# Moving a feed-forward in front of a top-k selection, into the loop of the norm before it

## What is computed

```python
h = h + attention(layernorm(h))
n = layernorm(h)
weights = n @ wr + br                        # one number per token
idx = top_k(weights, S // 2)[:S // 2 - 1]    # per batch element
y = gelu(n[idx] @ w1 + b1) @ w2 + b2         # 64 -> 256 -> 64
processed = zeros_like(n).at[idx].set(y * weights[idx])
out = h + processed + n
```

## Time and profile before

| | us |
|---|---|
| median of 3 runs | 5121.56 |
| lowest and highest | 5119.72, 5126.37 |
| the profiled execution | 5121.87 |
| its span | 5120.3 |
| second norm, selection, feed-forward within it | 242.6, 68.2, 263.8 |

### The profile page before, as it was taken

The page is one execution under the profiler, slowest core; times in us unless marked ns, Lnnn a source line. Parts: engine busy times, 40 slices in busy tenths (PEclk is TensorE's granted clock), DMA queues, the critical chain, the costliest instruction groups (busy, mean ns, idle before and its releaser), DMA issues. The chain is left out here.

```text
span 5120.3 us, 108154 instructions
## 1 busy us (share of the span) xinstructions
PE 4427.8 (86%) x42924; PEld 1534.1 (30%) x42924; DVE 3914.3 (76%) x4567; ACT 3520.9 (69%) x7159; POOL 592.9 (12%) x1086
## 2 busy tenths in 40 slices
PE   8888874999999889999998999999899999956366
PEld 2333321333333323333332333333233333311122
DVE  3444446899899879989997998999799899954511
ACT  4444440888888778888887888888788788832133
POOL 1222220100110010010001101100100010012100
PEclk9999985999999999999998999999899999977688
DMA  4333322000100010010001001000100100024233
GB/s 126 97 101 92 97 78 71 20 8 6 38 10 6 8 38 8 6 36 10 8 6 38 10 6 35 10 8 6 38 8 8 33 13 7 7 84 143 64 101 104
DMA packets 178692, 203.94 MB, mean 40 GB/s; under 512 B 55372, under 2 KB 138620, under 8 KB 177916
## 3 DMA queue, kind: packets, MB, share of 16 engines
q1 hardware_dynamic: 175444, 192.19, 13.7%
q10 hardware_dynamic: 2736, 4.76, 0.3%
HBM read 116.96 MB, written 79.02 MB: 38 GB/s over the span
## 5 line engine op out<-in xcount | busy, mean ns | idle before, releaser
L883 DVE TENSOR_REDUCE part_max<-max_scores 128x2 f32<-128x1024 f32 (+3 forms) x3096 | 3228.2, 1101 | 372.6 <-PE max_scores L841 270.3
L1011 ACT ACTIVATE probs<-scores 128x512 f32<-128x512 f32 (+4 forms) x6272 | 2997.7, 538 | 548.3 <-PE scores L1041 439.6
L1065 PE MATMUL out_acc<-probs,v_keys 128*32 128x256 f32 (+2 forms) x23424 | 1790.5, 378 | 0.0
L841 PE MATMUL max_scores<-k_rows,q_rows 48*128 48x512 bf16 (+5 forms) x6416 | 1148.3, 370 | 186.0 <-DVE part_max L883 116.0
L1041 PE MATMUL scores<-q_rows,k_rows 50*128 50x512 bf16 (+4 forms) x6272 | 1216.1, 354 | 92.1 <-ACT probs L1011 44.1
L991 POOL TENSOR_SCALAR_AFFINE_SELECT probs<-probs 128x256 f32<-128x256 f32 (+1 forms) x832 | 334.5, 402 | 3422.5 <-ACT probs L1011 3420.6
L841 PEld LDWEIGHTS max_scores<-k_rows,q_rows 48*128 48x128 bf16 (+1 forms) x6416 | 303.1, 94 | 1298.9 <-DVE part_max L883 762.9
L1065 PEld LDWEIGHTS out_acc<-probs,v_keys 128*32 128x32 f32 x23424 | 463.2, 108 | 736.5 <-issue 622.9
L1041 PEld LDWEIGHTS scores<-q_rows,k_rows 50*128 50x128 bf16 x6272 | 469.8, 94 | 435.2 <-ACT probs L1011 226.2
L570 ACT ACTIVATE gate<-gate_ps,b_sb 128x448 f32<-128x448 f32 x252 | 148.1, 631 | 285.9 <-PE gate_ps L483 265.3
L848 PE MATMUL max_scores<-masks_sb 64*128 64x128 bf16 (+2 forms) x3424 | 220.1, 207 | 0.0
(11 more groups left out here) (122 smaller groups left out, 2239.4 us busy)
## 6 DMA issues: line engine op xcount, KB each, us to landing
q_terms_dram<-q_st SPq DMA_DIRECT2D x168, 112.0 KB
q_rows<-q_terms_dram SPq DMA_DIRECT2D x180, 96.0 KB, 2.2
v_keys<-v_blocks_dram SPq DMA_DIRECT2D x18, 832.0 KB, 9.5
v_blocks_dram<-v_st SPq DMA_DIRECT2D x24, 512.0 KB, 3.5
x_taps<-in_x SPq DMA_DIRECT2D x96, 116.0 KB, 2.9
k_rows<-k_terms_dram SPq DMA_DIRECT2D x36, 306.0 KB, 7.1
k_terms_dram<-k_st SPq DMA_DIRECT2D x168, 56.0 KB
h_dram<-h SPq DMA_DIRECT2D x28, 224.0 KB, 2.0
```

Source lines behind the costliest of these rows:

```text
L841: last = nc.tensor.matmul(max_scores[to:to + m, n % M_RING, v, 0:keys], q_rows[rows, g, p, q0:q0 + m], k_rows[rows, (u // BU) % STEP_B, g, ...
L883: nc.vector.tensor_reduce(part_max[0:m, u % 2, i, :, p, c], max_scores[0:m, n % M_RING, :, 0:keys], AX_X, ALU.max).then_inc(max_used, 1)
L1011: nc.scalar.activation(probs[0:keys, k % P_RING, s, o:width[t]], scores[0:keys, (GH * k + s) % S_RING, o:width[t]], ACT.Exp, scale=float(H ...
L1065: last = nc.tensor.matmul(out_acc[VW * s:VW * s + VW, lo:hi], v_keys[0:keys, u // BU, g, j, v * VW:(v + 1) * VW], probs[0:keys, k % P_RING ...
```

## The change

The two loops of two steps become one unrolled loop over all 28 tiles, and the feed-forward goes into it. `second_norm` becomes `second_half`: it no longer stores `normed` and `total`; `total` stays in SBUF for all tiles (`total_all`), and the Gelu and both products of the feed-forward are done while the tile is there. The first product now takes 64 rows of each half, without zeros. Its result with the bias stays in SBUF too (`y_all`). The router's bias moves from ACT to DVE, the weights are stored tile by tile, and the constants' loads come behind those of the first two tiles. `proj_ps`, `var_ps` and `router_ps` go from two buffers to one. `select` is the same. `apply_chosen` takes the place of `feed_forward`: `chosen` comes in eight large loads ahead of all stores, DVE multiplies and adds, PE turns, ACT copies, SP stores.

```diff
+        hidden = sbuf("hidden3", [P, 2, 2, 2, TILE])
+        proj_ps = psum("proj2_ps", [P, TILE])
         centred_ps = psum("centred2_ps", [P, 2, TILE])
+        var_ps = psum("var2_ps", [P, TILE])
+        router_ps = psum("router_ps", [2, TILE])
+        hidden_ps = psum("hidden3_ps", [P, 2, TILE])
+        y_ps = psum("y3_ps", [P, TILE])
...
+            def _(sp):
...
+                load(0)
+                load(1)
...
+                for dst, src in pieces:
+                    sp.dma_start(dst, src).then_inc(const_in, 16)
+                for m in range(2, RING):
+                    load(m)
+                for m, (q, t0, w) in enumerate(ALL_TILES):
+                    if m + RING < NT:
+                        load(m + RING)
+                    sp.wait_ge(router_set, m + 1)
+                    sp.dma_start(weights_out[2 * q:2 * q + 2, t0:t0 + w], router[:, m % RING, 0:w]).then_inc(router_out[m % RING], 16)
...
+                def first(m, half):
+
+                    w = ALL_TILES[m][2]
+                    pe.wait_ge(normed_ready, m + 1)
+                    for e in range(2):
+                        n = 4 * m + 2 * half + e
+                        if n >= 2:
+                            pe.wait_ge(gelu_ready, n - 1)
+                        nc.tensor.matmul(hidden_ps[:, e, 0:w], w1_sb[C * e:C * (e + 1), half],
+                                         normed[C * e:C * (e + 1), m % RING, 0:w],
+                                         start=True, stop=True).then_inc(hidden_ready, 1)
+
+                def second(m):
+                    w = ALL_TILES[m][2]
+                    if m >= 1:
+                        pe.wait_ge(y_set, m)
...
+                pe.wait_ge(const_in, 16 * CONSTS)
+                project(0)
+                centre_tile(0)
+                project(1)
+                for m in range(NT + 2):
+                    if m < NT:
+                        variance(m)
+                    if 1 <= m <= NT:
+                        first(m - 1, 0)
+                    if m + 1 < NT:
+                        centre_tile(m + 1)
+                    if m + 2 < NT:
+                        project(m + 2)
+                    if m >= 2:
+                        second(m - 2)
+                    if 1 <= m <= NT:
+                        first(m - 1, 1)
+                        route(m - 1)
...
+                squares(0)
+                for m in range(NT + 1):
+                    if m < NT:
+                        deviation(m)
+                    if m >= 1:
+                        gelu(m - 1, 0)
+                    if m + 1 < NT:
+                        squares(m + 1)
+                    if m >= 1:
+                        gelu(m - 1, 1)
...
+                def take_up(m):
+                    q, t0, w = ALL_TILES[m]
+                    dve.wait_ge(y_ready, m + 1)
+                    nc.vector.tensor_scalar(y_all[:, q, t0:t0 + w], y_ps[:, 0:w], b2_sb[:], None, ALU.add).then_inc(y_set, 1)
+
+                def weigh(m):
+                    w = ALL_TILES[m][2]
+                    dve.wait_ge(router_ready, m + 1)
+                    if m >= RING:
+                        dve.wait_ge(router_out[m % RING], 16 * (m // RING))
+                    nc.vector.tensor_scalar(router[:, m % RING, 0:w], router_ps[:, 0:w], br_sb[:], None, ALU.add).then_inc(router_set, 1)
...
+                    if m + 2 < NT:
+                        residual(m + 2)
+                    if m >= 2:
+                        take_up(m - 2)
+                    if 1 <= m <= NT:
+                        weigh(m - 1)
...
+def apply_chosen(nc, y_all, total_all, chosen_in, identity, out):
...
+        MIDDLE = 4 * TILE
...
+            def _(sp):
+                for q in range(PAIRS):
+                    for part, (a, b) in enumerate(((0, MIDDLE), (MIDDLE, S))):
+                        rows = chosen_in[2 * q:2 * q + 2][:, None, a:b]
+                        sp.dma_start(chosen[:, q, a:b], rows.to_broadcast([2, C, b - a])).then_inc(loaded[2 * q + part], 16)
...
+                for m, (q, t0, w) in enumerate(ALL_TILES):
+                    r = m % RING
+                    sp.wait_ge(turned_set, m + 1)
+                    k, rest = divmod(w, P)
+                    for e in range(2):
+                        rows = out[2 * q + e]
+                        sp.dma_start(rows[t0:t0 + k * P].rearrange("(k p) c -> p k c", p=P),
+                                     turned[:, r, 0:k, e * C:(e + 1) * C]).then_inc(stored[r], 16)
...
+                    dve.wait_ge(loaded[2 * q + (t0 >= MIDDLE)], 16)
+                    nc.vector.tensor_tensor(scaled[:, m % 2, 0:w], y_all[:, q, t0:t0 + w], chosen[:, q, t0:t0 + w],
+                                            ALU.mult).then_inc(scaled_ready, 1)
...
+                    act.wait_ge(turned_ready, m + 1)
+                    if m >= RING:
+                        act.wait_ge(stored[r], stored_by(m, r))
```

More of the change, by code:

```diff
@@ L1185, in second_norm @@
         router_set = sem("router_set")
[L1186 to L1237, removed]
-                        if m >= 2:
[L1239 to L1269, removed]
-                        nc.gpsimd.tensor_tensor(attn[:, m % 2, 0:w], heads[:, r, 0:w], inv[:, r, 0:w],
-                                                ALU.mult).then_inc(attn_ready, 1)
-                    def add(m):
-                        w = STEP_TILES[m][2]
-                        r, left, count = tile_out(m)
-                        pool.wait_ge(normed_ready, m + 1)
-                        if m >= RING:
-                            pool.wait_ge(left, count)
-                        nc.gpsimd.tensor_tensor(total[:, r, 0:w], normed[:, r, 0:w], h2[:, r, 0:w],
-                                                ALU.add).then_inc(total_ready, 1)
-                    multiply(0)
-                    multiply(1)
-                    for m in range(NT):
-                        if m + 2 < NT:
-                            multiply(m + 2)
-                        if m >= 1:
-                            add(m - 1)
-                    add(NT - 1)
-                @block.vector
-                def _(dve):
-                    def residual(m):
-                        w = STEP_TILES[m][2]
-                        dve.wait_ge(proj_ready, m + 1)
-                        r, landed, count = tile_in(m)
-                        dve.wait_ge(landed, count)
-                        if m >= RING:
-                            dve.wait_ge(total_ready, m - RING + 1)
-                            dve.wait_ge(centred, m - RING + 1)
-                        nc.vector.tensor_tensor(h2[:, r, 0:w], proj_ps[:, m % 2, 0:w], h0[:, r, 0:w],
-                                                ALU.add).then_inc(h2_ready, 1)
-                    residual(0)
-                    residual(1)
-                    for m in range(NT):
-                        w = STEP_TILES[m][2]
@@ L1522, in feed_forward @@
         turned_set = sem("turned3_set")
-        stored = [sem("out3_stored_even"), sem("out3_stored_odd")]
-        step_sems = [*loaded, hidden_ready, gelu_ready, y_ready, scaled_ready, final_ready, turned_ready,
-                     turned_set, *stored]
-        NT = len(STEP_TILES)
+        stored = [sem(f"out3_{r}_stored") for r in range(RING)]
+        NT = len(ALL_TILES)
         def stores(m):
-            w = STEP_TILES[m][2]
+            w = ALL_TILES[m][2]
             return 2 * ((w >= P) + (w % P > 0))
-        def stored_by(m, half):
-            return 16 * sum(stores(n) for n in range(m) if n % 2 == half)
@@ L1680, in program @@
     inverse_sums(nc, heads, inverse)
[L1681 to L1683 removed]
+    with nc.sbuf_tensor("y_all", [P, PAIRS, S], F32) as y_all, nc.sbuf_tensor("total_all", [P, PAIRS, S], F32) as total_all:
+        second_half(nc, heads, inverse, h0, a["wo"], a["wr"], a["br"], (a["centre"], a["mean"]),
+                    (a["ff_w1"], a["ff_w2"]), (a["ff_b1"], a["ff_b2"]), y_all, total_all, weights)
+        select(nc, weights, a["batch_sum"], a["batch_before"], chosen)
+        apply_chosen(nc, y_all, total_all, chosen, a["identity"], out)
 def arranged(i):
@@ L1735, in arranged @@
     same = at[:, None] // ROWS_PER_BATCH == at[None, :] // ROWS_PER_BATCH
-    ff_w1 = np.zeros((2, C, CHUNKS, P), np.float32)
-    for e in range(2):
-        for half in range(2):
-            ff_w1[e, :, 2 * e + half] = i["L0_ffn_w1"][:, half * P:(half + 1) * P]
     return {
```

402 lines of the change are left out of this document (185 added, 217 removed).

## The result

The changed kernel takes 5004.6 us, median of 4 runs (5003.3 to 5006.9), against 5120.9 us: a ratio of 0.977, 95% interval 0.976 to 0.979. The forecast was 5006 us. The profiled run took 5004.5 us, span 5002.4 us.

A forecast was written before the change was run, and what follows sets the result against it. A queue round of loads and stores bound the second norm, two DMA engines the feed-forward. Span 5120.3 - 20.6 (loop) - 94.8 (last stage) = 5004.9 us, with 1.57 us above span 5006 us; its own range 4973 to 5046.

The forecast's parts named there:

- Bound of the second norm: Second norm before the change: a queue round of POOL's add, SP's store, next load and POOL's multiply, 8.54 us per tile.
- bound of the feed-forward: Feed-forward before the change: loads of `chosen` run on two DMA engines, 8.1 us per full tile, 207 of 263.8 us.
- Last stage, 169 us: Stage after selection: loads 129 us plus stores 31.5 us on two engines, plus ends; 169 us against 263.8, gain 94.8.
- the line through two packet sizes: Last stage's loads: packet cost 9.8 ns + 0.0371 ns a byte, from 256 B and 2048 B packets; 129 us in all.
- 31.5 + 8: Last stage beyond its loads: stores 31.5 us, then 1 us to first byte, 3 us ring refill, 4 us last copy and store.
- The loop, 222 us: Merged loop: PE sets 7.2 us a full tile, 5.0 a short one, 193 us plus ends; 222 against 242.6, gain 20.6.
- Start and end: Loop outside its rounds: 18.8 us to the first variance, some 2 us at low clock, 8 us behind the last round.
- Rival 1, the table switch: Loop: a table switch stalls ACT as long again as its load, 9.2 us a tile; kernel 5063 us, chance 0.07.
- Rival 2, spread loads: Last stage: the larger loads of `chosen` spread over all engines, about 25 us; kernel 4897 us, chance 0.06.
- Rival 3: Loop: PE stays at its low clock, 0.50, with a round of 14.0 us; kernel 5160 us, chance 0.04.
- Rival 4: Loop stays bound by its loads, round 8.5 us, POOL waiting each round; kernel 5027 us, chance 0.83 together with the forecast.
- the almost two rounds of room: Loop: SP's loads are wanted almost two rounds later, so 5.45 + 1.26 us fit into 2 x 7 us.

## Why the prediction was right

- *Bound of the second norm, bound of the feed-forward.* Both named rightly; taking away the one alone gave 64 us and the other alone 68 us, and they add.
- *Last stage, 169 us.* The loads came to 129 us as forecast: the line through two packet sizes held at 8 KB on two engines, and the stores stood behind them. The rest took 36 us where 31.5 + 8 were put; the surplus of 4 us is most likely the ends, put too long. That the order of the two does not change their sum is not shown: with the order changed the stage took 170 us, but ACT's issue set its end. SP's issue did not pace the stores: in the changed kernel they ran at 86% of the engines.
- *The loop, 222 us.* Right that PE sets the round; the size of the round was off. I counted 0.43 us a pass without drain and 0.2 us for all hand-overs, though in the earlier trace rows the eight passes take 4881.71 - 4878.08 = 3.63 us from start to start, 0.45 each. The seven groups of a round start 0.94 to 1.06 us apart for every two passes that I put at 0.86, so a full round is 7.91 us and not 7.2. A pair of seven tiles takes 4692.10 - 4640.81 = 51.3 us by SP's stores, where 6 x 7.2 + 5.0 = 48.2 were put: 12 us too few over four pairs, with a short tile at 51.3 - 6 x 7.91 = 3.8 us in place of 5.0. Start and end had been put at 29 us and took 225.9 - 205.2 = 20.7 us, 8 too many, so the sum missed by only 4. That these two offset, and then the loop's 4 us and the last stage's, is luck: without it 5006 would not have met 5004.6 so closely. `take_up` and `weigh` were a little short too, 0.74 us each for 0.66 to 0.68, which DVE, at work in 120.6 of 160 us, does not feel. That the first and last rounds are shorter, since they lack the parts of tiles not there, is argued and not measured.
- *Rival 1, the table switch:* no gap behind the loads, and without the switches the kernel's time stays the same within its interval (ratio 0.978 against 0.977). The Trainium skill, page "ScalarE: Activation LUTs", section "What ACT_TABLE_LOAD costs", has a drain of 1.38 us beside each load; the trace has 0.01 us between load and next operation, so that the measurement decides against it here.
- *Rival 2, spread loads:* false for the change as made (12.6%), and true as an edit: the 4897 us worked out for it became 4907.8 when the load was spread by hand.
- *Rival 3:* the granted clock in the loop was 1.00.
- *Rival 4:* its sign did show, but not its time. POOL waits for `h_tile` in every round:

```profile
4697.65 1.27 POOL L1346 TENSOR_TENSOR attn<-heads,inv_rows 128x512 f32<-128x512 f32 x1 [6.46 <-DMA h_tile<-h_dram]
...
4701.14 1.02 PE L1231 MATMUL proj_ps<-attn,wo_sb 128*128 128x512 f32 x2
```

PE takes up `attn` 2.2 us after POOL ends it, 1.3 to 3 us with the other full tiles, so the round does not wait. But these loads are issued from 4692.45 on, when POOL has waited for them since 4691.19: the almost two rounds of room that the prediction gave them are in truth those few microseconds.

## What to carry to other kernels

Look at the DMA share of a slow load before restructuring around it: one near 1/8 of 16 engines means that two of them do the work, and splitting the transfer is a two-line edit of the order of the restructuring: 68 us in the kernel before and 97 in the changed one, where the change itself gave 116. When a stage is bound by a loop through queues, try the order of the DMA issues first, and then compare the restructured kernel with the mended old one, not with the old one. A busy share of 100% on PE does not say that PE never waits, since a row can take a wait in; compare a row's length with its like in other rounds, and shorten PE's work and, by itself, its neighbour's.

## What the hardware did that was not expected

- *Clock.* The granted clock stayed at 0.50 (1.2 GHz) in 60 us in which PE was never idle, with products of 2 rows and transposes of 128 columns; in the loop, as busy, it was 1.00 (2.4 GHz) over 160 us.
- *DMA rate.* Two engines bring 53 GB/s of packets of 8 and 4.9 KB, 26 GB/s each; all 16 bring 225 GB/s, 14 each, at a share of 1.0. Writing both partition halves at once leaves it at 226. The 16 engines carried 356 GB/s elsewhere in the same program; whether the repeated source row or the 64 partitions of each transfer hold the rate of `chosen` wasn't tried and stays open.
- *Small stores beside large loads.* Issued from another queue, a pair of 128 KB stores held its issuing engine up to 25.7 us while two of the 16 engines were full of 8 KB packets.
